# A two-layer graph network on one core: first output layer ahead of the segment sum, and a row tile scattered earlier

## The reference, cut to what matters

```python
h = jnp.maximum(_layernorm(x, axis=-1), 0.0)
# attention: self loops and edges, softmax over the edges of a destination
x_l, x_r = h @ W_l + b_l, h @ W_r + b_r
...
out = jax.ops.segment_sum(alpha[:, :, None] * x_l[s], d, num_segments=N)
x = x + out.reshape(N, H * C) + bias

h = jnp.maximum(_layernorm(x, axis=-1), 0.0)
Wij = (shifted_softplus(f_ij @ Wf1 + bf1) @ Wf2 + bf2) * rcut_ij[:, None]
msg = (h @ W_in2f)[idx_j] * Wij
agg = jax.ops.segment_sum(msg, idx_i, num_segments=n_atoms)
x = x + shifted_softplus(agg @ Wo1 + bo1) @ Wo2 + bo2
```

## Time and profile before

| | |
|---|---|
| median of the runs | 3588.07 us (3582.42 to 3593.24) |
| span of the profiled execution, first to last instruction | 3550.3 us |
| what lies around it, against the median run | 37.8 us |
| busy: PE, DVE, ACT, POOL | 82%, 75%, 64%, 53% of the span |
| granted clock of TensorE, mean | 0.918 |
| DMA | 545.65 MB, mean 154 GB/s |

### The profile page before, as it was taken

One profiled execution on the slowest core, in us unless ns is written; L12 is line 12 of the kernel. 1 busy time (PEld: TensorE's weight loads), 2 busy tenths in 40 slices (PEclk: granted clock), 3 DMA queues, 4 the chain that ended last, 5 costly groups with the idle time before them and its releaser, 6 DMA issues.

```text
span 3550.3 us, 60748 instructions
## 1 busy us (share of the span) xinstructions
PE 2925.4 (82%) x16576; PEld 1746.4 (49%) x16576; DVE 2674.8 (75%) x7105; ACT 2271.7 (64%) x4705; POOL 1874.7 (53%) x1583
## 2 busy tenths in 40 slices
PE   3999968888888888897777777777777775999999
PEld 2666644444444444443444444444444443666665
DVE  5888859999999999999676676667667664444454
ACT  3999956666666666665555555555555553888887
POOL 0000046666666666663688888888888886000000
PEclk9999989999999999999877888878888887999999
DMA  4767733333333333333455555555555555777776
GB/s 169 254 246 251 248 112 121 122 125 112 125 125 110 127 122 112 126 122 104 105 109 108 108 108 112 108 106 110 108 108 108 111 107 116 278 291 291 294 294 236
DMA packets 280365, 545.65 MB, mean 154 GB/s; under 512 B 96723, under 2 KB 173037, under 8 KB 242639
## 3 DMA queue, kind: packets, MB, share of 16 engines
q1 hardware_dynamic: 186255, 447.94, 37.2%
q0 software_dynamic: 94080, 97.34, 15.4%
HBM read 317.71 MB, written 235.91 MB: 156 GB/s over the span
## 4 chain that ended last, share of the span: by engine, by line
DVE 30%; issue 21%; PE 18%; POOL 12%; ACT 9%; DMA 9%; SPq 1%; POOLq 1%; DVEq 0%; ACTq 0%
POOL sum_dram L567 7%; PE bank L1368 6%; ACT d_n L983 6%; PE bank L1359 5%; POOL x_dram L555 4%; DMA b_x<-x_end_dram 4%; DVE a_sum L818 3%; DVE a_max L780 3%; PE bank L1174 3%; DMA x_dram<-b_x,sidx 3%; DVE stat_e_six L750 2%; DVE a_nd L761 2%; DVE a_pv L812 2%; PE bank L1208 2%; PE bank L1365 2%
## 5 line engine op out<-in xcount | busy, mean ns | idle before, releaser
L529 POOL DMA_INDIRECT a_xs<-in_x,gidx x392 | 399.6, 1019 | 589.7 <-issue 589.7
L567 POOL DMA_INDIRECT sum_dram<-b_sum,b_at x392 | 616.6, 1573 | 137.8 <-issue 118.6
L535 POOL DMA_INDIRECT a_xd<-in_x,gidx x392 | 408.8, 1043 | 241.4 <-DVE a_base L797 150.6
L555 POOL DMA_INDIRECT x_dram<-b_x,sidx x392 | 443.3, 1131 | 158.8 <-issue 138.4
L934 DVE SCALAR_TENSOR_TENSOR f_ssp_out<-bank,cols,f_ln_out 128x512 f32<-128x512 f32 x196 | 147.1, 751 | 295.2 <-ACT f_ln_out L1082 295.2
L597 ACT ACTIVATE stat_e_log<-stat_e_var 128x8 f32<-128x8 f32 (+1 forms) x196 | 40.5, 207 | 507.3 <-DVE stat_e_var L593 507.3
L850 DVE BATCH_NORM_STATS2 stat_e_six<-b_x 128x6 f32<-128x128 f32 x392 | 85.5, 281 | 357.1 <-DMA b_x<-x_end_dram 357.1
L1328 PE MATMUL bank<-b_rows,b_same 128*128 128x128 bf16 x4704 | 331.8, 240 | 0.2 <-ACT b_sum L1125 0.2
L1328 PEld LDWEIGHTS bank<-b_rows,b_same 128*128 128x128 bf16 x4704 | 317.0, 110 | 0.3 <-issue 0.3
L983 ACT ACTIVATE d_n<-d_x,stat_d_shift,stat_d_rstd 128x128 f32<-128x128 f32 x686 | 283.5, 485 | 0.2 <-DVE stat_d_shift L603 0.2
L1174 PE MATMUL bank<-ident,d_n 128*128 128x128 f32 x1568 | 229.6, 275 | 43.9 <-DMA d_n<-sum_dram 29.5
(11 more groups left out here) (174 smaller groups left out, 7193.6 us busy)
## 6 DMA issues: line engine op xcount, KB each, us to landing
d_x<-in_x SPq DMA_DIRECT2D x49, 1024.0 KB, 6.8
x_dram<-d_x SPq DMA_DIRECT2D x49, 1024.0 KB, 4.8
d_n<-sum_dram SPq DMA_DIRECT2D x49, 1024.0 KB, 6.9
d_x<-x_dram SPq DMA_DIRECT2D x49, 1024.0 KB, 8.8
out<-d_x SPq DMA_DIRECT2D x49, 1024.0 KB, 4.9
sum_dram<-zero SPq DMA_DIRECT2D x48, 1024.0 KB, 5.5
x_end_dram<-a_x SPq DMA_DIRECT2D x98, 256.0 KB, 3.5
b_x<-x_end_dram SPq DMA_DIRECT2D x98, 256.0 KB
```

What stands on the lines that cost most here:

```text
L529: pool.indirect_dma_start(a_xs[s][:, j * F:(j + 1) * F], None, x, bass.IndirectOffsetOnAxis(ap=gidx[s][:, j:j + 1], axis=0)).then_inc(src_ ...
L535: pool.indirect_dma_start(a_xd[s][:, j * F:(j + 1) * F], None, x, bass.IndirectOffsetOnAxis(ap=gidx[s][:, 4 + j:5 + j], axis=0)).then_inc( ...
L555: pool.indirect_dma_start(x1_dram, bass.IndirectOffsetOnAxis(ap=sidx[s][:, j:j + 1], axis=0), b_x[s][:, j * F:(j + 1) * F], None, bounds_c ...
L567: pool.indirect_dma_start(sum_dram, bass.IndirectOffsetOnAxis(ap=b_at[s][:, j:j + 1], axis=0), b_sum[s][:, j * F:(j + 1) * F], None, compu ...
```

## The change

The first output layer goes ahead of the segment sum. In the edge stage the turn of the message becomes a product with Wo1, so `sum_dram` holds agg @ Wo1. The output stage then turns the sums and takes abs with bo1 at once: copy, first layer and their semaphores go. The constant part of the last layer (bo2 and the log 2 term, `bo_row`) is added to every node row ahead: for all rows in the input stage's bias (`bias_d3`), and for scattered rows by DVE, in `a_xo` and `b_xo`. The bias product of the output stage goes.

Each chunk's first row tile is scattered in the attention stage (`early_scatters`, from `a_xo`), the other three in the edge stage (from `b_xo`, reversed slots). Scatters read `b_xo` instead of `b_x`, so the load of `b_x` waits for DVE's addition (`b_xo_ready`), no longer for the scatter.

POOL's index columns are read in place from `index`, and its loops are written out. The sums have four slots in the output stage (two of them in the place of the edge stage's tiles), turns and second layers have four banks each, and the second layer follows its turn after two passes instead of three. The load of the first node rows is issued before the wait for the last adds.

```diff
+EARLY = (1, 1)
...
+        with ExitStack() as place:
+            f_sums = d_n + [at(f"f_sums{i}", [P, J * F]) for i in range(RX - RN)]
...
+            const(bo2_all[:, :], bo2.rearrange("(a f) -> a f", a=1).broadcast_to([P, F]))
...
-            def load_gidx(k, u):
+            def step_a(k, u, t0, keep=True, end=True):
+
                 s = u % 2
-                sp.dma_start(gidx[s][:, :], index[:, bass.ds(12 * (2 * k + u), 8)]).then_inc(gidx_loaded[s], 16)
...
-                if gather:
-                    sp.wait_ge(src_gathered[s], 64 * turn(k, u))
-                    sp.wait_ge(dst_gathered[s], 64 * turn(k, u))
-                    load_gidx(k, u + 2)
...
-                    sp.wait_ge(x1_scattered[s], 64 * turn(k, u - 2))
+                    sp.wait_ge(b_xo_ready, t - 1)
                     sp.sem_inc(sync_step, 1)
                     sp.wait_ge(b_norm, t - 1)
                     sp.sem_inc(sync_step, 1)
                 sp.dma_start(b_x[s][:, :], x1_end_dram[bass.ds(NC - 1 - t, 1), :, :].rearrange("o p f -> (o p) f")).then_inc(b_x_ld[s], 16)
-                sp.dma_start(sidx[s][:, :], index[:, bass.ds(12 * (NC - 1 - t) + 8, 4)]).then_inc(b_sidx_ld[s], 16)
...
-                sp.wait_ge(x1_scattered[s], 64 * HALF)
-                sp.wait_ge(added[s], 64 * HALF)
+                sp.wait_ge(x1_scattered[s], late(s) * HALF)
             def load_sums(g, slot):
-                sp.dma_start(d_n[slot % RN][:, :], node_rows(sum_dram, g)).then_inc(f_sum_ld[slot % RN], 16)
+                sp.dma_start(f_sums[slot][:, :], node_rows(sum_dram, g)).then_inc(f_sum_ld[slot], 16)
             def load_x1(g, slot):
                 sp.dma_start(d_x[slot][:, :], node_rows(x1_dram, g)).then_inc(f_x1_ld[slot], 16)
             def step_f(g, slot, more=True):
-                if more or g + RN < NG:
+                if more or g + RX < NG:
                     sp.wait_ge(f_turned, QUADS * g + QUADS)
-                    load_sums(g + RN, slot)
+                    load_sums(g + RX, slot)
                 if more or g + RX - 1 < NG:
                     load_x1(g + RX - 1, (slot - 1) % RX)
                 sp.wait_ge(f_out, QUADS * g + QUADS)
                 sp.dma_start(node_rows(out, g), d_x1[slot % RN][:, :]).then_inc(out_stored[slot % RN], 16)
-            for g in range(RN):
+            load_x1(0, 0)
+            for s in range(2):
+                sp.wait_ge(added[s], 64 * HALF)
+            for g in range(RX):
                 load_sums(g, g)
-            for g in range(RX - 1):
-                load_x1(g, g)
+                if 0 < g < RX - 1:
+                    load_x1(g, g)
...
+            def column(t, n):
+                return bass.IndirectOffsetOnAxis(ap=index[:, 12 * t + n:12 * t + n + 1], axis=0)
+
+            def gathers(t):
+                s = t % 2
+                if t >= 2:
+                    pool.wait_ge(norm_src, t - 1)
                     pool.sem_inc(pool_step, 1)
                 for j in range(TILES):
-                    pool.indirect_dma_start(a_xd[s][:, j * F:(j + 1) * F], None, x,
-                                            bass.IndirectOffsetOnAxis(ap=gidx[s][:, 4 + j:5 + j], axis=0)).then_inc(dst_gathered[s], 16)
-
-            for u in range(4):
-                gathers(0, u, u)
-            with pool.Fori(2, HALF) as k:
-                for u in range(2):
-                    gathers(k, u, 4)
-
+                    pool.indirect_dma_start(a_xs[s][:, j * F:(j + 1) * F], None, x, column(t, j)).then_inc(src_gathered[s], 16)
+                if t >= 2:
+                    pool.wait_ge(base_ready, t - 1)
+                    pool.sem_inc(pool_step, 1)
+                for j in range(TILES):
+                    pool.indirect_dma_start(a_xd[s][:, j * F:(j + 1) * F], None, x, column(t, TILES + j)).then_inc(dst_gathered[s], 16)
+
+            def early_scatters(t):
+                s = t % 2
+                pool.wait_ge(early_ready, t + 1)
+                pool.sem_inc(pool_step, 1)
+                for j in range(EARLY[s]):
+                    pool.indirect_dma_start(x1_dram, column(t, 2 * TILES + j), a_xo[s][:, j * F:(j + 1) * F], None,
+                                            bounds_check=bound, oob_is_err=False).then_inc(early_scattered[s], 16)
             for i in range(RN):
                 pool.wait_ge(x1_stored[i], 16 * in_slot[i])
+                pool.sem_inc(pool_step, 1)
+            for t in range(NC + 4):
+                if t < NC:
+                    gathers(t)
+                if t >= 4:
+                    early_scatters(t - 4)
...
+            def scatters(t):
+                s = t % 2
+                pool.wait_ge(b_xo_ready, t + 1)
                 pool.sem_inc(pool_step, 1)
-                for j in range(TILES):
-                    pool.indirect_dma_start(x1_dram, bass.IndirectOffsetOnAxis(ap=sidx[s][:, j:j + 1], axis=0),
-                                            b_x[s][:, j * F:(j + 1) * F], None,
+                for j in range(EARLY[1 - s], TILES):
+                    pool.indirect_dma_start(x1_dram, column(NC - 1 - t, 2 * TILES + j), b_xo[s][:, j * F:(j + 1) * F], None,
                                             bounds_check=bound, oob_is_err=False).then_inc(x1_scattered[s], 16)
...
+            for t in range(NC + 2):
+                if t < NC:
+                    scatters(t)
+                if t >= 2:
+                    adds(t - 2)
...
+            dve.tensor_scalar(bo1_all[:, :], ident[:, :], 0.0, cols[:, 5:6], ALU.mult, ALU.add)
...
-            dve.tensor_tensor(part3[:, 0, F:2 * F], rows3[:, 2 * F:3 * F], bank[3][0:3, 0:F], ALU.add)
+            for j in range(TILES):
+                dve.tensor_tensor(bo_row[:, j * F:(j + 1) * F], bo2_all[:, :], bank[3][:, 0:F], ALU.add)
             link(dve.tensor_tensor(part3[:, 0, 0:F], rows3[:, 0:F], rows3[:, F:2 * F], ALU.add))
+            link(dve.tensor_tensor(part3[:, 0, F:2 * F], bo_row[0:3, 0:F], part3[:, 0, 0:F], ALU.add))
...
+                if back:
+                    dve.wait_ge(x1_ready, t - 1)
+                    if t0 >= 4:
+                        dve.wait_ge(early_scattered[s], 16 * EARLY[s] * turn(k, u - 4))
+                    dve.tensor_tensor(a_xo[s][:, 0:early(s)], a_x1[s][:, 0:early(s)], bo_row[:, 0:early(s)], ALU.add).then_inc(early_ready, 1)
...
+                if t0 >= 2:
+                    dve.wait_ge(x1_scattered[s], late(s) * turn(k, u - 2))
+                dve.tensor_tensor(b_xo[s][:, early(1 - s):], b_x[s][:, early(1 - s):], bo_row[:, early(1 - s):], ALU.add).then_inc(b_xo_ready, 1)
...
-            def f_copy(c, q, c0):
+            def f_abs_of(c, q):
+
                 act.wait_ge(f_turned, c + 1)
-                if c0 >= 2:
-                    act.wait_ge(f_z, c - 1)
-                act.activation(turned[q % 2][:, :], bank[q % 2][:, :], ACT.Copy).then_inc(f_copied, 1)
-
-            def f_network(c, q, c0, between=lambda: None):
+                act.activation(f_abs_out[q % 2][:, :], bank[q][:, :], ACT.Abs, bias=cols[:, 5:6]).then_inc(f_abs, 1)
+
+            def f_network(c, q, c0, ahead=True):
+
+                act.wait_ge(f_abs, c + 1)
+                act.activation(f_exp_out[q % 2][:, :], f_abs_out[q % 2][:, :], ACT.Exp, scale=-1.0).then_inc(f_exp, 1)
+                if ahead:
+                    f_abs_of(c + 1, (q + 1) % QUADS)
+                act.wait_ge(f_exp, c + 1)
                 if c0 >= 2:
                     act.wait_ge(f_s, c - 1)
-                softplus(bank[2 + q % 2], f_abs_out, f_exp_out, f_ln_out[q % 2], f_z, f_abs, f_exp, f_ln, c + 1,
-                         bias=cols[:, 5:6], between=between)
-
-            def f_group(g, g0):
+                act.activation(f_ln_out[q % 2][:, :], f_exp_out[q % 2][:, :], ACT.Ln, scale=0.5, bias=0.5).then_inc(f_ln, 1)
...
-                pe.matmul(to[:, :], ones3[:, 0:P], bias3[:, :, :].rearrange("k j f -> k (j f)"), start=True, stop=False)
+                pe.matmul(to[:, :], ones3[:, 0:P], bias_d3[:, :, :].rearrange("k j f -> k (j f)"), start=True, stop=False)
...
-                    turn_tiles(bank[5], b_msg).then_inc(b_msg_turned, 1)
+                    for j in range(TILES):
+                        last = pe.matmul(bank[5][:, j * F:(j + 1) * F], b_msg[:, j * P:(j + 1) * P], wo1[:, :],
+                                         start=True, stop=True)
+                    last.then_inc(b_msg_turned, 1)
...
-                    pe.wait_ge(f_sum_ld[slot % RN], 16 * (RX // RN * m + slot // RN + 1))
-                if c0 >= 2:
-                    pe.wait_ge(f_copied, c - 1)
-                turn_tiles(bank[q % 2], d_n[slot % RN][:, q * 512:(q + 1) * 512]).then_inc(f_turned, 1)
-
-            def f_first(c, q, c0):
-                pe.wait_ge(f_copied, c + 1)
-                if c0 >= 2:
-                    pe.wait_ge(f_s, c - 1)
-                to = bank[2 + q % 2]
-                pe.matmul(to[:, :], wo1[:, :], turned[q % 2][:, :], start=True, stop=True).then_inc(f_z, 1)
```

(14 more changed lines are left out.)

128 lines of the change are left out of this document (51 added, 77 removed).

## The result

| | |
|---|---|
| before, four runs | 3590.65 us median (3582.42 to 3595.02) |
| changed, four runs | 3668.73 us median (3656.89 to 3683.14) |
| ratio | 1.0227, 95% interval 1.0197 to 1.0256: slower, by about 2% |
| profiled execution of the changed kernel | span 3654.1 us, own time 3656.89 us |

A forecast was written before the change was run, and what follows sets the result against it. Bounds before: DVE in attention, POOL in edge (13.20 us a chunk), PE in output. Span 3550.3 - 136 + 22 - 116 + 2.5 = 3322.8 us, plus 37.8 us, gives 3361 us, 6.3% faster; range 3315 to 3445 us.

The forecast's parts named there:

- the price of the early scatter: Attention stage: one more scatter and one DVE addition a chunk cost +22 us, bounds +20 and +50.
- my rivals: PE clock falls (0.14, 3390 us); second edge bound (0.12, 3440); DMA engines not filled (0.10, 3400); slower than before (0.03).
- the straight list: Rival, attention and edge stages: POOL's 1568 unlooped DMAs each cost more, slower from 0.15 us each; chance 0.03.
- 37.8 us above the profiled span: Whole kernel: gap between median run and profiled span, kept as a constant and added to the forecast span.
- Output stage: Limit moves from PE to the DMA engines, 8.6 us a group instead of 10.81; 547.1 to 431 us, -116 us.
- my lower bound: Output stage: 8.1 us a group, from two loads at 442 GB/s and a store at 317 GB/s.
- The start and end of the stage: Output stage: 10 us for the first load and the last tiles, on top of 49 groups.
- Edge stage: One scatter fewer takes POOL from 13.20 to 11.77 us a chunk; 95 x 1.43 = -136 us.
- No new wait arises: Edge stage: three scatters, 4.3 us, between two chunks' adds cover POOL's 2.67 us wait for adds to land.
- the new two-input addition: DVE's bias-row addition charged POOL nothing; the skill's contention rule, about 0.29 us each, would add some 57 us.
- Sum: Whole kernel: -136 edge, +22 attention, -116 output, +2.5 setup and handovers, giving a span of 3322.8 us.
- the signs I had named: Right if 294 edge scatters, chunk 11.8 us, attention chunk 12.2 us, output DMA share 0.95 or more, clock 1.00.

The follow-up runs named there:

- e16: Kernel before, unedited, repeated for its trace on a chip of the slower sort, which shows stops; profiled span 3594.6 us.
- e2: Kernel before with POOL's attention-stage loop written out as a straight list and SP's small index loads there removed; 3565.91 us against 3587.58 us for before.
- e11: Changed kernel, unedited, on a chip where the kernel before takes about 3556 us; 3323.85 us, ratio 0.9343.
- e14: Changed kernel with a ninth gather into a spare tile replacing the early scatter, all four tiles scattered in the edge stage; span 3447.2 us.
- e1: Changed kernel without the early scatter, its addition and waits; all four tiles scattered in the edge stage; span 3440.1 us.
- e17: Unedited repeat of e1, the changed kernel without the early scatter; span 3440.3 us, ratio 0.962 of before.
- e8: Changed kernel with POOL filling a 128x1024 spare tile where the early scatter stood, all four tiles scattered in the edge stage; span 3565.2 us.
- e5: Changed kernel with SP's 49 stores of zeros to the sums issued in the dense input stage instead of the attention stage; span 3675.8 us.

## Why the prediction was wrong, and where it was right

**The step that failed** is the price of the early scatter: "I take +22 us with bounds of +20 (DVE alone) and +50". I had counted POOL's idle time of 1.60 us a chunk as room to be filled, and called POOL and DVE level. On sort I this is exact: 1226 us against 1203, and a chunk is 12.21 us where I had 12.20 by DVE. On sort II it is +335 us, the result against e16. What stood in its place was not a longer instruction: with the ninth transfer POOL's pause is gone, and then PE, ACT and DVE stop for 5 to 9 us, mostly every second chunk. Why they stop stays open. The rows named ahead show POOL issue at most eight gathers before a pause. The trace shown ahead does hold 36 in a row at the start of the stage, but without a stop, so it could not have warned me; e16 could. In the edge stage POOL goes on without a pause at a slower pace, and I took that as proof that a saturated POOL is harmless. An unseen condition deserved a bound from above, and had none. None of my rivals was this one; the straight list, my one case of "slower", costs nothing (e2).

**The clue I passed over.** "The median run stands 37.8 us above the profiled span, which I keep." In every later run the own time is less than 4 us above the span. The trace I had read fits sort I (3550.3 us beside about 3556, and its number of semaphore records), the times I had been given fit sort II. The constant was most likely no overhead but the difference between two sorts of chip.

**The other terms**, measured in e11 against the trace of before:

- *Output stage*, predicted -116, measured -166 us. The mechanism is right: DMA share 1.01, PE 85% and ACT 91% busy, clock 1.00. Missized was the group: 7.44 us by the starts of ACT's abs instead of 8.6, under my lower bound of 8.1. That bound took two loads at 442 and one store at 317 GB/s, which is 390 GB/s on the mean; together they run at 423. The start and end of the stage take 17 us, not 10. By the Trainium skill, "DMA: Bandwidth & Descriptors", section Specifications, HBM limits a core to about 358 GB/s. The trace of e11 does not agree: it is at 423 GB/s over 250 us.
- *Edge stage*, predicted -136, measured -88 us. POOL has its 294 scatters at 1.10 us; a chunk is 12.27 us by the starts of the new addition from the fourth on, not 11.77. e14, on the same chip as e11, is in this stage the changed kernel with four scatters instead of three, and so separates the two parts of the 48 us. From before to e14 the stage grows from 1322 to 1360 us: +38 us, which I had put at nothing. From e14 to e11 the fourth scatter goes: -126 us, near to my -136. The groups of the kernel before, e14 and e11:

```profile
L567 POOL DMA_INDIRECT sum_dram<-b_sum,b_at x392 | 616.6, 1573 | 137.8 <-issue 118.6 <-ACT b_sum L1125 16.6 <-DMA sum_dram<-b_sum,b_at 2.7
```

```profile
L583 POOL DMA_INDIRECT sum_dram<-b_sum,b_at x392 | 654.1, 1669 | 133.5 <-issue 112.2 <-ACT b_sum L1146 9.8 <-DVE b_xo L873 6.4
```

```profile
L583 POOL DMA_INDIRECT sum_dram<-b_sum,b_at x392 | 644.5, 1644 | 164.3 <-issue 99.4 <-DMA sum_dram<-b_sum,b_at 42.7 <-ACT b_sum L1146 14.0
L570 POOL DMA_INDIRECT x_dram<-b_xo,index x294 | 323.0, 1099 | 104.7 <-issue 84.5 <-DVE b_xo L873 15.7 <-DMA sum_dram<-b_sum,b_at 4.6
```

  The 38 us are the longer adds: 1669 ns each in e14 against 1573, 0.38 us a chunk. In e11 they are 1644 ns, which is 28 us over the stage. The other part in e11 is the wait for the previous chunk's adds to land. The gap before a chunk's first add is 0.66 us on the mean, where it is 0.30 before and in e14, so it costs about 34 us; of the 42.7 us in the row, 0.30 each time are the usual gap. "No new wait arises" was wrong: three scatters cover less of it than four. I had charged POOL nothing for the new two-input addition. By the Trainium skill, "GPSIMD Engine Reference", section Specifications, it should hold a POOL transfer. The trace agrees in size: the adds of e11 are longer by 4 x 0.07 = 0.28 us a chunk, close to the 0.29 us I had worked out for one such hold, and they go with the addition's width (128x384 in e11, 128x512 in e14). But no run has the new stage without the addition, so that it is the cause is not shown. In the attention stage it costs nothing on the path on sort I.
- *Sum.* +23, -88, -166 and +2 make -229; I had -227.5. On sort I the forecast span was 3322.8 us and the measured one 3320.4. Two terms were off by 50 us and cancelled, so the agreement is partly luck.

Of the signs I had named, most are there on both sorts: 294 scatters, DVE idle before the new addition, DMA share over 0.95, clock 1.00 in the output stage. The attention chunk of 12.2 us is there on sort I alone (12.21), and its absence is what showed the fault.

## What to carry to other kernels

Idle time of an engine that is off the critical path may be doing something: before filling the last microsecond of a pause, look whether any trace shows that engine without it, at that pace. When all engines thin out together, compare the end of the work with the end of the wait for it before you look for a bound, and count the trace's records before you trust the releaser that it names. And when a profiled span and the run times differ by more than the runs spread, they may not be of one chip: settle that first, and repeat every surprising run beside the original on one chip. The form without the early scatter (e1, e17) gains 4% on sort II and was not run on sort I; there e14, which differs from it in the addition and a ninth gather that it does not need, takes 3449.96 us, so it should be near that and behind the changed kernel. Which of the two to keep depends on where it must run.

## What the runs showed of the hardware that I had not expected

- Two sorts of chip, or two states of it, 0.9% apart on the kernel before, and 10% apart (3668.73 against 3323.85 us) on the changed one.
- On one sort, when 17 or 18 indirect transfers of POOL follow in a row, 1.29 us apart on the median, waits on PE's work end 6 to 8 us late in the stop that I read, and an issue of SP takes 0.7 instead of 0.33 us, though the DMA engines are busy 29% on the mean there. The traces of that sort lack about half of the semaphore records, and only in the two stages with indirect transfers (e16). Which of these causes which is not known.
- The DMA engines sustain 423 GB/s in a mixture of two loads and one store (e11).
- A fill of 128x1024 by POOL (0.96 us) makes four VectorE operations beside it take 2.37 us instead of 1.09 (e8, e11).
- The 49 stores of zeros, 1 MB each, have no part in the stops, and moved to the input stage they lengthen it by 21 us (e5).
